# An eight-layer attention, spline and expert model on one core: cutting on TensorE, a split spline, dense work for 256 tokens

## The reference

```python
logits = h @ router_w
expert_idx = jnp.argmax(logits, axis=-1)
for e in range(E):
    gv = h @ expert_wv[e]
    gate_raw, value = jnp.split(gv, 2, axis=-1)
    y = gate_raw * jax.nn.sigmoid(gate_raw) * value @ expert_proj[e]
    out = out + jnp.where((expert_idx == e)[..., None], y, 0.0)
```

## Time and profile before

| | before |
|---|---|
| median of 3 runs | 2485.65 us (2482.36 to 2489.24) |
| the profiled execution | 2488.74 us |
| its span | 2487.0 us |
| PE busy | 1956.2 us, 79% |
| DVE busy | 1734.1 us, 70% |
| ACT busy | 1338.5 us, 54% |
| POOL busy | 416.4 us, 17% |
| mean granted TensorE clock | 0.893 |

### The profile page before, as it was taken

How to read it: one execution, slowest core, us unless ns; L and a number is a source line. 1 busy time by engine, 2 the same in 40 slices (tenths; PEclk the granted TensorE clock), 3 DMA queues, 4 the chain that set the end, 5 groups by cost and what they waited for, 6 DMA issues and landing times. The chain is left out here.

```text
span 2487.0 us, 38310 instructions
## 1 busy us (share of the span) xinstructions
PE 1956.2 (79%) x12778; PEld 851.6 (34%) x12778; DVE 1734.1 (70%) x4426; ACT 1338.5 (54%) x1901; POOL 416.4 (17%) x668
## 2 busy tenths in 40 slices
PE   3589999994679964864899999949445899999836
PEld 2122333233434443551223332238231233332336
DVE  6688788747567776566887888532786887887423
ACT  3246666674379955333366666722532466666712
POOL 4001021020055521300001210132000000100132
PEclk8699999996889986886999999969766999999958
DMA  7700120001111100017002100014026010100034
GB/s 196 157 1 10 31 40 1 1 2 41 51 49 47 47 10 0 1 30 191 17 1 40 23 18 1 2 50 167 20 71 167 1 22 20 40 1 1 1 98 155
DMA packets 67603, 113.41 MB, mean 46 GB/s; under 512 B 12596, under 2 KB 49588, under 8 KB 66692
## 3 DMA queue, kind: packets, MB, share of 16 engines
q1 hardware_dynamic: 59696, 97.54, 14.4%
q0 software_dynamic: 4768, 10.26, 1.4%
q10 hardware_dynamic: 2976, 3.55, 0.6%
HBM read 63.34 MB, written 30.18 MB: 38 GB/s over the span
## 5 line engine op out<-in xcount | busy, mean ns | idle before, releaser
L1032 ACT ACTIVATE probs<-score 128x1024 f32<-128x1024 f32 x960 | 825.7, 897 | 538.8 <-PE score L1096 535.5
L1154 DVE TENSOR_REDUCE max_part<-stat 128x1 f32<-128x512 f32 x1152 | 721.5, 682 | 126.4 <-PE stat L1046 124.9
L1109 PE MATMUL pv<-probs,v_ones 128*9 128x512 f32 (+3 forms) x3840 | 443.8, 534 | 0.7 <-ACT out_turned L1023 0.5
L1151 DVE CUSTOM_DVE_ANT_0 masked_scores<-stat,mask_row 128x128 f32<-128x128 f32 (+3 forms) x768 | 343.0, 487 | 105.5 <-PE stat L1046 104.0
L1006 POOL TENSOR_SCALAR_AFFINE_SELECT probs<-probs 128x256 f32<-128x256 f32 x384 | 154.5, 408 | 1264.5 <-ACT probs L1032 1261.0
L1046 PE MATMUL stat<-first_group_k,first_group_q 128*128 128x512 bf16 (+2 forms) x960 | 303.1, 371 | 78.1 <-DVE max_part L1154 33.8
L1046 PE MATMUL stat<-group_k,group_q 128*128 128x512 bf16 (+2 forms) x960 | 288.4, 349 | 14.9 <-DVE max_part L1154 8.8
L1096 PE MATMUL score<-first_group_q,first_group_k 128*128 128x512 bf16 x960 | 262.8, 357 | 24.8 <-DMA first_group_q<-row_max_turned 23.7
L1096 PE MATMUL score<-group_q,group_k 128*128 128x512 bf16 x960 | 254.0, 350 | 5.1 <-DMA group_q<-row_max_turned 2.8
L1046 PEld LDWEIGHTS stat<-first_group_k,first_group_q 128*128 128x128 bf16 x960 | 94.0, 99 | 261.4 <-DVE max_part L1154 122.9
L1755 ACT ACTIVATE abs_act_ps<-abs_act_ps 128x1024 f32<-128x1024 f32 (+3 forms) x176 | 167.5, 952 | 27.3 <-PE abs_act_ps L1708 27.1
(11 more groups left out here) (355 smaller groups left out, 2274.0 us busy)
## 6 DMA issues: line engine op xcount, KB each, us to landing
tile_wv<-expert_wv SPq DMA_DIRECT2D x38, 512.0 KB, 3.0
q_parts<-parts_t SPq DMA_DIRECT2D x40, 384.0 KB, 3.9
group_k<-k_parts SPq DMA_DIRECT2D x18, 384.0 KB
group_q<-q_parts SPq DMA_DIRECT2D x18, 384.0 KB
k_parts<-parts_t SPq DMA_DIRECT2D x16, 384.0 KB, 4.5
head_q<-q_parts SPq DMA_DIRECT2D x48, 96.0 KB
head_k<-k_parts SPq DMA_DIRECT2D x48, 96.0 KB
first_group_k<-k_parts SPq DMA_DIRECT2D x9, 384.0 KB
```

Of the source, the lines that this page charges most:

```text
L1032: nc.scalar.activation(probs[:, n % PSLOTS, :, 0:width], sc[hp][:, :, 0:width], ACT.Exp, scale=scale).then_inc(expd.sem, 1)
L1109: last = nc.tensor.matmul(acc[32 * h:32 * h + D + 1, f:BANK], v9[:, kt, g * HG + h, :], probs[:, (2 * t + h // 2) % PSLOTS, h % 2, 0:BANK ...
L1151: nc.vector.tensor_tensor_reduce(masked[:, at % 2, 0:width], ring[n % RBANKS][:, 0:width], w["mask_row"][:, BANK - width:BANK], 1.0, NEG, ...
L1154: nc.vector.reduce_max(into, ring[n % RBANKS][:], AX.X).then_inc(stat_used.sem, 1)
```

## The change

- **Parts.** The turns are now plain matmuls with the identity, on top of a PSUM tile that was first set to zero by a matmul of minus identity with zeros. ScalarE copies part 0 as bf16, TensorE subtracts that part from PSUM (minus identity in bf16, `take_out`), ScalarE copies part 1, and so on; VectorE's two subtractions and `rest` are gone. Part 2 of a block is taken after part 0 of the next. Of the last block VectorE copies the keys' parts, ScalarE the queries'.
- **Four buffers** of parts instead of two. SP stores blocks 0 to 2 in the projection stage. The last block's stores, block 1's rows and the first norm (twelve activations before ScalarE's shift rows, four after) are moved into the attention stage. There the stores of the last block are split over SP and ScalarE, and SP issues the shift rows before it waits for the stores and loads the other columns, queries too.
- `Norm`'s four turns stand ahead of the first projection; the first two convolutions stand behind the last normalised rows.
- **Spline** by 512 columns: 32 knots of 512, eight knot buffers, even and odd h in sums of their own that are joined at the end; the first column block is completed while the second is summed.
- **Experts.** Fewer, wider pick steps. Only the first 14 token tiles are sorted, so 17 slot tiles. The last two token tiles go through all four experts (16 chunks of gate and value of 128 channels x 256 tokens, then the projections), between the routing and the first sorted tile; VectorE adds each expert's result times its pick to x. x + y is moved ahead of the logits. POOL scatters a tile of ones into rows of the output buffer that are written again later, before it waits for the slots.
- Some counters get shared names, and three small tiles of the norm are allocated once.

The diff, cut to its core:

```diff
-SLOTS = NT + E - 1
+DENSE = 2
+SLOTS = NT - DENSE + E - 1
...
                 def turn(c):
+                    if c == 1:
+                        pe.wait_ge(norm.kept.sem, norm.kept.at(NQ))
+                    if c >= 2:
+                        pe.wait_ge(cut[PARTS - 1].sem, cut[PARTS - 1].at(c - 1))
+                    for s in range(2):
+                        nc.tensor.matmul(tp[c % 2][:, s, :], w["minus16"][:], zeros, start=True, stop=True)
                     pe.wait_ge(ready.sem, ready.at(c + 1))
-                    if c == 1:
-                        norm.wait(pe, NQ - 1)
-                    if c >= 2:
-                        pe.wait_ge(rested.sem, rested.at(c - 1))
                     for s in range(2):
                         for i in range(QC):
-                            ins = nc.tensor.transpose(tp[c % 2][:, s, i * P:(i + 1) * P], qkv[:, QC * c + i, s * C:(s + 1) * C], w["ident"][:])
+                            ins = nc.tensor.matmul(tp[c % 2][:, s, i * P:(i + 1) * P], qkv[:, QC * c + i, s * C:(s + 1) * C], w["ident"][:],
+                                                   start=False, stop=True, skip_group_check=True)
                     ins.then_inc(turned.sem, 1)
 
-                norm.turn(pe, 0)
-                norm.turn(pe, 1)
+                def take_out(c, a):
+
+                    pe.wait_ge(cut[a].sem, cut[a].at(c + 1))
+                    for s in range(2):
+                        if c == NQ - 1 and s == 1:
+                            pe.wait_ge(keys_cut.sem, keys_cut.at(a + 1))
+                        ins = nc.tensor.matmul(tp[c % 2][:, s, :], w["minus16"][:], parts[c][:, s, a, :], start=False, stop=True, skip_group_check=True)
+                    ins.then_inc(taken[a].sem, 1)
+
+                for n in range(NQ):
+                    norm.turn(pe, n)
                 project(0)
-                norm.turn(pe, 2)
-                norm.turn(pe, 3)
                 project(1)
                 for n in range(NQ):
                     turn(n)
+                    if n > 0:
+                        take_out(n - 1, 1)
                     if n + 2 < NQ:
                         project(n + 2)
+                    take_out(n, 0)
+                take_out(NQ - 1, 1)
...
+                def part(c, a):
+                    if a == 0:
+                        act.wait_ge(turned.sem, turned.at(c + 1))
+                    else:
+                        act.wait_ge(taken[a - 1].sem, taken[a - 1].at(c + 1))
+                    if c < NQ - 1:
+                        ins = nc.scalar.copy(parts[c][:, :, a, :], tp[c % 2][:])
+                    else:
+                        ins = nc.scalar.copy(parts[c][:, 0, a, :], tp[c % 2][:, 0])
+                    ins.then_inc(cut[a].sem, 1)
+
                 for n in range(NQ):
-                    act.wait_ge(turned.sem, turned.at(n + 1))
-                    if n >= 2:
-                        act.wait_ge(stored[n - 2].sem, stored[n - 2].at(NS))
-                    nc.scalar.copy(turned_sb[:, n % 2, :, 0, :], tp[n % 2][:]).then_inc(first_cut.sem, 1)
+                    part(n, 0)
                     if normed and n + 1 < NQ:
                         root(n + 1)
+                    if n > 0:
+                        part(n - 1, 2)
                     if not biased and n + 2 < NQ:
                         evacuate(n + 2)
                         if normed:
                             square(n + 2)
-                    act.wait_ge(rested.sem, rested.at(n + 1))
-                    nc.scalar.copy(turned_sb[:, n % 2, :, 1, :], rest[:, n % 2]).then_inc(second_cut.sem, 1)
-                    if norm.twice:
-                        norm.first_norm(first_norm, n)
-                if rows:
-                    load_rows(act, 1)
+                    part(n, 1)
+                part(NQ - 1, 2)
...
-                    sp.wait_ge(last_cut.sem, last_cut.at(c + 1))
-                    cols = slice(c * BANK, (c + 1) * BANK)
-                    for copy in range(PARTS if rows else 1):
-                        sp.dma_start(parts_dram[0][:, :, copy, cols].rearrange("a p t -> p a t"), turned_sb[:, c % 2, 0]).then_inc(stored[c].sem, 16)
-                    sp.dma_start(parts_dram[1][:, :, cols], turned_sb[:, c % 2, 1]).then_inc(stored[c].sem, 16)
+                for c in range(NQ - 1 if rows else NQ):
+                    sp.wait_ge(cut[PARTS - 1].sem, cut[PARTS - 1].at(c + 1))
+                    for copy in range(COPIES):
+                        store_q(sp, c, copy)
+                    if c < NQ - 1:
+                        store_k(sp, c)
                     if rows and c == 1:
-                        load_rows(sp, 0)
+                        sp.wait_ge(stored[0].sem, stored[0].at(NS))
+                        load_k(sp, rows[1], parts_dram[1], 0, range(PARTS), slice(0, BANK), begun)
+                        load_q(sp, rows[0], parts_dram[0], 0, range(PARTS), slice(0, BANK), begun)
+                for c in range(2):
+                    sp.wait_ge(stored[c].sem, stored[c].at(NS))
...
+                sp.wait_ge(stored[1].sem, stored[1].at(0))
+                load_k(sp, uk[0], parts_dram[1], 0, range(PARTS), slice(BANK, 2 * BANK), begun[1])
+                load_q(sp, uq[0], parts_dram[0], 0, range(PARTS), slice(BANK, 2 * BANK), begun[1])
+                for copy in range(PARTS - 1):
+                    store_queries(sp, parts_dram, NQ - 1, copy, last_parts, stored[NQ - 1])
+                load_shift(0)
                 wait_parts(sp, stored)
                 load_k(sp, uk[0], parts_dram[1], 0, range(PARTS), OTHER_COLS, loaded[0])
-                load_shift(0)
+                load_q(sp, uq[0], parts_dram[0], 0, range(PARTS), OTHER_COLS, loaded[0])
...
-                wait_parts(act, stored)
-                load_q(act, uq[0], parts_dram[0], 0, range(PARTS), OTHER_COLS, loaded[0])
+                store_keys(act, parts_dram, NQ - 1, last_parts, stored[NQ - 1])
+                store_queries(act, parts_dram, NQ - 1, PARTS - 1, last_parts, stored[NQ - 1])
                 act.wait_ge(v_cleared.sem, v_cleared.at(1))
                 nc.scalar.copy(v9[:, :, :, 0:D], v[:, :, 2 * C:3 * C].rearrange("p t (h d) -> p t h d", d=D)).then_inc(v_ready.sem, 1)
+                if first_norm:
+                    for c in range(NQ - 1):
+                        first_norm(c)
                 act.wait_ge(stat_used.sem, stat_used.at(shift_at(0) + 1))
                 load_shift_rows(act, 0, range(HG // 2, HG))
+                if first_norm:
+                    first_norm(NQ - 1)
...
+                def bend(c, h):
+                    n = c * INNER + h
+                    if h == 0:
+                        act.wait_ge(s_ready.sem, s_ready.at(c + 1))
+                    if n >= SLOTS:
+                        act.wait_ge(summed.sem, summed.at(n - SLOTS + 1))
+                    nc.scalar.activation(knot[:, n % SLOTS, :], s2[:, c, :], ACT.Relu, bias=w["b1"][:, h:h + 1],
+                                         scale=w["W1"][:, h:h + 1]).then_inc(knots.sem, 1)
+
+                def begin(n):
+                    if n == 1:
+                        enter(0)
+                        for h in range(2):
+                            bend(0, h)
+
+                norm.act(act, begin)
+                for h in range(2, INNER):
+                    bend(0, h)
+                    if h == 3:
+                        enter(1)
                 for h in range(INNER):
-                    if h >= 4:
-                        act.wait_ge(summed.sem, summed.at(h - 3))
-                    nc.scalar.activation(knot[:, h % 4, :], s2[:], ACT.Relu, bias=w["b1"][:, h:h + 1],
-                                         scale=w["W1"][:, h:h + 1]).then_inc(knots.sem, 1)
+                    bend(1, h)
                 load_roots(k, w)
...
+                def add(c, h):
+                    n = c * INNER + h
+                    dve.wait_ge(knots.sem, knots.at(n + 1))
+                    into = g[:, c, h % 2, (h // 2) % 2, :]
+                    if h == 0:
+                        ins = nc.vector.tensor_scalar(into, knot[:, n % SLOTS, :], w["W2"][:, 0:1], w["b2"][:, 0:1], ALU.mult, ALU.add)
+                    elif h == 1:
+                        ins = nc.vector.tensor_scalar(into, knot[:, n % SLOTS, :], w["W2"][:, 1:2], None, ALU.mult)
+                    else:
+                        dve.wait_ge(summed.sem, summed.at(n - 1))
+                        ins = nc.vector.scalar_tensor_tensor(into, knot[:, n % SLOTS, :], w["W2"][:, h:h + 1], g[:, c, h % 2, (h // 2 - 1) % 2, :], ALU.mult, ALU.add)
+                    ins.then_inc(summed.sem, 1)
...
+                pool.wait_ge(ranked.sem, ranked.at(1))
+                nc.gpsimd.indirect_dma_start(out_dram, bass.IndirectOffsetOnAxis(ap=h[:, 0, C:C + 1].bitcast(I32), axis=0), ones[:], None).then_inc(returned.sem, 16)
+                pool.wait_ge(returned.sem, returned.at(16))
```

(34 more changed lines are left out.)

308 lines of the change are left out of this document (180 added, 128 removed).

## The result

The changed kernel took 2448.59 us (median of 4 executions, 2446.39 to 2455.15) against 2486.36 for the kernel before: ratio 0.9854, 95% interval 0.983 to 0.9877. It is faster, as forecast, but by 38 us instead of 83, and outside the range of 2385 to 2438.

A forecast was written before the change was run, and what follows sets the result against it. Attention's steady part was taken as TensorE-bound and untouched, the rest as stages in series. Gains of 13.9 + 16.1 + 14.3 + 5.9 + 7.4 + 25.0 = 82.6 us from 2485.65 gave 2403 us, range 2385 to 2438.

The forecast's parts named there:

- Projections: Four projection stages: VectorE loses its subtractions and TensorE takes them over; norm 8.2, retention 5.9, rope 11.0 us each.
- Rope: Two rope projection stages: 8.9 us won up to the last rotation and 2.1 in the tail, each.
- tail: Rope projection, last rotation to attention: 9.2 us instead of 11.3, 2.1 won, with ten SP issues counted.
- Retention: Retention's projection: TensorE becomes the bound at 8.3 us per block; 4.8 us won in three intervals, 1.1 in the tail.
- Attention's start: Start of three attention stages: row-max DMA issued ahead of the row loads, saving waits of 5.7, 5.1 and 3.3 us.
- needed some 12 us later: 0 to 4: Attention's start: other columns' loads issued at about 10 us instead of 5; loss of 0 to 4 us, taken as 0.
- Rival B: Attention starts: small DMA finds block 3's stores in front, starts gain nothing, 14.1 us back, 2417; chance 0.12.
- Splines: Two spline stages in 512-column halves: earlier first knot, fewer output matmuls behind the last sum; 3.7 us each, 7.4 together.
- 1.5 us of stall before the second half arrives: Spline: first knot starts 4.2 us earlier on half the input, less 1.5 us waiting for the other half.
- pace: Spline sums: 32 steps at 0.70 us, 22.4 us instead of 21.8, so 0.6 us lost.
- Experts: Two expert stages: shorter picks, faster and fewer sorting DMAs, dense work in TensorE's idle time, fewer tiles; 12.5 us each.
- rival A: Expert stages: dense block runs at half clock, 16 us more each, 2435; chance 0.12.

The follow-up runs named there:

- r1: The changed kernel run again in a later series, nothing altered: 2431.25 us, ratio 0.9772.
- a1: Changed kernel, but SP issues the second unit's row maxima ahead of the pads and loads of the second group: 2415.5 us, ratio 0.9704.
- c2: Kernel of a1, with SP's half of the first unit's row-max DMA put back behind the other columns' loads: 2418.11 us.
- c1: Kernel before the change, with SP's second row-max DMA issued ahead of the second group's pads and loads: 2472.89 us.
- a4: Changed kernel, but in the splines ScalarE normalises all four rows ahead of the first copy: 2446.41 us.
- a3: Changed kernel, but POOL starts its 14 sorting DMAs only when the dense block is done: 2480.39 us, one execution.
- a2: Changed kernel, but SP's first four expert weight loads are issued behind the loads of the sorted rows: 2445.8 us, ratio 0.9831.
- b1: Changed kernel with one tile of 128 tokens through the dense block instead of two: 2440.68 us.

## Why the prediction was right or wrong

**Projections: right in sum, with two terms that offset each other.** Forecast 36.1 us for the four; measured 39.1 (first series) and 37.0 (r1). Rope gained 12.1 and 13.4 instead of 11.0: up to the last rotation 12.0 and 12.7 instead of 8.9, for the blocks came 0.5 us closer and the last one more, but in the tail only 0.1 and 0.7 instead of 2.1, since SP had 14 DMAs to issue and not ten. That the two cancelled is luck. Retention gained 4.5 instead of 5.9: 7.0 ahead of the last turn, but its tail, where 1.1 was to be won, became 2.4 longer. TensorE did become the bound in retention (38.1 of 44 us busy), at nearly full clock (0.93); in rope VectorE went on without a gap as well.

**Attention's start: wrong, 22 us.** This is the step that failed: "The row maxima come back through a small DMA ... Now it is issued ahead of them ... so I take the waits nearly whole: 5.7, 5.1, 3.3". The first unit's DMA behaved so. But I followed the queue for one DMA only. The next of the same kind, one unit later, lay behind everything that had been pushed back: block 3's stores, unit 1's rows, the other columns, the second group. I had given "needed some 12 us later: 0 to 4 ... taken as 0, since the issues end well ahead": the issues do (1138.8), the bytes do not (the DMA behind them is used at 1167.66). Measured +2.9, +2.2 and +3.7 us where 14.1 in all were to be won. Rival B named the right place with the wrong mechanism, and its worst outcome, nothing gained, was not bad enough. a1 shows the wait that was missing, c2 that the first DMA's place matters only with it out of the way; c1 adds that bulk behind an urgent DMA may slow it as well, which the forecast's queue did not have either.

**Splines: wrong, 7 us.** The first sum starts 7.3 us into the stage instead of 12.0 (4.7 won, forecast 4.2), and the last sum lies 7.2 us ahead of the end instead of 10.2 (3.1 won). But from first to last sum it is 28.4 us instead of 21.9, 6.5 lost where the forecast had 3.7 (stall 1.5, pace 0.6, joining 0.7, completes 0.9). The mis-sized term is the stall, "1.5 us of stall before the second half arrives": VectorE waited 2.5 us before the third knot, and the sum behind it lasted 1.9 us longer than the others (2.3 in the second stage), as POOL's addition of `bout` ran beside it: 4.4 us for the 1.5. In the kernel before that addition was over at 575.16, ahead of the first sum at 577.76; starting the sums earlier put them under it, and the forecast has no term for that. The joins were two, 1.3 us, and completes and statistics 2.0; the pace was better than forecast, 0.66 us a sum instead of 0.70, and won 1.1 where 0.6 was to be lost. a4 gives back 1.2 and 1.7.

**Experts: right in r1, wrong in the first series.** Forecast 12.5 each. r1 has 13.0 and 12.6, and the dense block ends as the rows arrive. In the first series 0.9 and 6.6: what stood in its way was neither rival A (the clock; each 256-column instruction took 0.22 us up to the stall, the full clock, and the 6 us at half clock follow it) nor anything in the rows of before, where no engine computed while POOL sorted. That this overlap is new could be read from the earlier trace rows; I took it as free.

With the delay (17.5 us short), attention (22.9), splines (7.0), and 5.7 better elsewhere, the miss against the span is 82.6 - 40.9 = 41.7. Without it, in r1, 82.6 - 55.1 = 27.5. The 2431.25 us of r1 lie inside the range of 2385 to 2438, though the attention starts were as wrong there as in the first series: that is the width of the range, whose upper end was made for rival A, and not the mechanism.

What is open: the cause of the delay. It went with POOL's sorting DMAs moved away (a3) and stayed with the weight loads moved away (a2). It was in every profile of two series whose dense block overlapped with the sorting, and in none of three later series; a1 to a4 and r1 ran on the same chip. The DMA engines' load does not tell the two apart. Windows from 24 to 30 and from 30 to 36 us into the first expert stage, the changed kernel in the first series, then r1 (columns as in the earlier trace rows):

```profile
1636.30:1642.30 6.00, 3.12 (x21) 2.56 (x19) 0.14 (x1) 0.00 (x0) 4.47 (x6) 1.00 0.74 270
1642.30:1648.30 6.00, 0.00 (x0) 0.00 (x0) 0.61 (x2) 0.38 (x1) 4.47 (x6) 0.54 0.14 44
```

```profile
1639.10:1645.10 6.00, 6.00 (x41) 5.45 (x40) 2.31 (x6) 1.53 (x4) 4.47 (x6) 1.00 0.75 274
1645.10:1651.10 6.00, 6.00 (x39) 5.39 (x39) 2.61 (x8) 1.53 (x4) 4.48 (x6) 1.00 0.14 47
```

They move the same bytes at the same time (270 and 274, then 44 and 47 GB/s), and POOL is equally busy; only ScalarE, VectorE and TensorE stand. Code loading is unlikely: in the first stage the instruction queues' packets come 17 and 21 us into it with the delay (the changed kernel, a1, a4) and without (c2, b1).
